# Non-local attention block: values to the output banks, outputs over six PSUM banks, pooled phi kept in theta's bank

## What is computed

```python
theta = jnp.einsum('bhwc,cd->bhwd', x, W_theta)            # 256 -> 32
phi = _maxpool2x2(jnp.einsum('bhwc,cd->bhwd', x, W_phi))   # 256 -> 32, pooled
g = _maxpool2x2(jnp.einsum('bhwc,cd->bhwd', x, W_g))       # 256 -> 128, pooled
theta = theta.reshape(B, S, Cc // 8)                       # S = 1024 pixels
phi = phi.reshape(B, Sk, Cc // 8)                          # Sk = 256 cells
g = g.reshape(B, Sk, Cc // 2)
beta = jax.nn.softmax(jnp.einsum('bqd,bkd->bqk', theta, phi), axis=-1)
tmp = jnp.einsum('bqk,bkv->bqv', beta, g).reshape(B, H, W, Cc // 2)
o = jnp.einsum('bhwv,vc->bhwc', tmp, W_o)
return gamma * o + x
```

## Time and profile before

| | us |
|---|---|
| median of 3 runs | 249.46 |
| lowest, highest | 247.31, 251.14 |
| the profiled execution | 248.0 |
| its span (first to last instruction) | 246.2 |
| TensorE busy | 235.7 (96%) |
| VectorE busy | 205.8 (84%) |
| GpSimd busy | 168.7 (69%) |
| ScalarE busy | 148.1 (60%) |

### The profile page before, as it was taken

One profiled execution on the slowest core, in us unless ns is written; L12 is line 12 of the kernel. 1 busy time (PEld: TensorE's weight loads), 2 busy tenths in 40 slices (PEclk: granted clock), 3 DMA queues, 4 the chain that ended last, 5 costly groups with the idle time before them and its releaser, 6 DMA issues.

```text
span 246.2 us, 4332 instructions
## 1 busy us (share of the span) xinstructions
PE 235.7 (96%) x1464; PEld 210.4 (85%) x1464; DVE 205.8 (84%) x473; ACT 148.1 (60%) x275; POOL 168.7 (69%) x119
## 2 busy tenths in 40 slices
PE   7896999999999999999999999999999999999884
PEld 4675888898989889898989989898998989899774
DVE  4587896988989898898989899898989989898855
ACT  3763865847475684847567484747749474735260
POOL 1596588676868677686958767695876779544480
PEclk9999999999999999999999999999999999999999
DMA  6790009549194775919377592928668391906924
GB/s 221 285 393 18 3 1 313 204 104 386 49 311 177 234 284 124 384 63 337 123 209 303 142 365 77 347 101 270 243 218 296 95 357 70 329 14 226 372 88 173
DMA packets 15078, 51.14 MB, mean 208 GB/s; under 512 B 1872, under 2 KB 2512, under 8 KB 15056
## 3 DMA queue, kind: packets, MB, share of 16 engines
q1 hardware_dynamic: 14368, 50.14, 58.2%
q10 hardware_dynamic: 688, 0.72, 0.8%
HBM read 33.95 MB, written 16.78 MB: 206 GB/s over the span
## 4 chain that ended last, share of the span: by engine, by line
PE 80%; DVE 7%; DMA 4%; ACT 3%; POOL 3%; issue 1%; ACTq 0%; DVEq 0%
PE proj L195 30%; PE out L299 24%; PE shift L299 8%; PE shift L272 6%; PE score L229 5%; PE score L256 4%; DVE neg_parts L577 3%; DMA x_t<-in_xt 2%; POOL e_lo L506 2%; DMA theta<-neg_lo 2%; PE shift L195 1%; DVE out L552 1%; DVE theta L558 1%; POOL x_lo L501 1%; PE proj L188 1%
## 5 line engine op out<-in xcount | busy, mean ns | idle before, releaser
L506 POOL TENSOR_TENSOR e_lo<-e_sb,e_hi 128x512 fp32r<-128x512 f32 x64 | 82.0, 1295 | 50.8 <-ACT e_sb L434 50.8
L501 POOL TENSOR_TENSOR x_lo<-x_t,x_hi 128x1024 fp32r<-128x1024 f32 x31 | 74.3, 2398 | 13.7 <-ACT x_hi L391 13.7
L299 PE MATMUL out<-G_hi,e_lo 128*128 128x258 f32 x188 | 53.2, 283 | 0.5 <-POOL e_lo L506 0.5
L299 PE MATMUL out<-G_hi,e_hi 128*128 128x258 f32 x188 | 53.4, 284 | 0.0
L299 PE MATMUL out<-G_lo,e_hi 128*128 128x258 f32 x188 | 53.3, 283 | 0.0
L603 DVE SCALAR_TENSOR_TENSOR y_sb<-out,r_sum,x_n 128x256 f32<-128x256 f32 x94 | 45.5, 484 | 6.4
L195 PE MATMUL proj<-x_hi,w_hi 128*128 128x512 f32 x122 | 48.4, 396 | 2.3 <-DVE theta L558 2.3
L195 PE MATMUL proj<-x_hi,w_lo 128*128 128x512 f32 x122 | 48.3, 396 | 0.0
L195 PE MATMUL proj<-x_lo,w_hi 128*128 128x512 f32 x122 | 48.2, 395 | 0.0
L431 ACT ACTIVATE e_hi<-shift 128x512 fp32r<-128x512 f32 x64 | 38.5, 601 | 13.5 <-PE shift L272 13.5
L577 DVE TENSOR_REDUCE neg_parts<-score 128x2 f32<-128x512 f32 x64 | 43.6, 685 | 1.3 <-PE score L229 0.4
(11 more groups left out here) (81 smaller groups left out, 386.3 us busy)
## 6 DMA issues: line engine op xcount, KB each, us to landing
x_n<-in_xn SPq DMA_DIRECT2D x32, 512.0 KB, 7.3
x_t<-in_xt SPq DMA_DIRECT2D x31, 512.0 KB, 5.3
out<-y_sb SPq DMA_DIRECT2D x31, 512.0 KB, 6.6
x_t<-in_xt ACTq DMA_DIRECT2D x2, 256.0 KB, 4.7
w_sb<-in_w_proj SPq DMA_DIRECT2D x1, 256.0 KB, 3.7
theta<-neg_hi ACTq DMA_DIRECT2D x16, 4.0 KB
theta<-neg_lo SPq DMA_DIRECT2D x16, 4.0 KB
out<-y_sb SPq DMA_DIRECT2D x1, 256.0 KB, 2.4
```

Of the source, the lines that this page charges most:

```text
L299: last = nc.tensor.matmul(out_bank(i, t)[:, 0:GW], e[:, i % 2, KC * h + k, cells], G[:, i % 3, k, :], start=(n == 0), stop=(n == 3 * KC - 1))
L501: nc.gpsimd.tensor_tensor(x_lo[:, i % 2, h], x_t[:, i % 2, h], x_hi[:, i % 2, h].bitcast(f32), ALU.subtract).then_inc(x_lo_ready, 1)
L506: nc.gpsimd.tensor_tensor(e_lo[:, i % 2, n, :], e_sb[:, n, :], e_hi[:, i % 2, n, :].bitcast(f32), ALU.subtract).then_inc(e_lo_ready, 1)
```

## The change

`values` go to `outb[h]` for all images but the first (before: `proj[h]`). The output tiles rotate over six banks (before: tiles 2 and 3 in `shift`, the others in `outb`). `mix` of images 0 and 1 goes to other banks. `phi_max` moves from rows 96 to 127 of `outb[1]` to rows 64 to 95 of `proj[0]`, where the third copy of theta was. Since ScalarE reads those rows in `theta_high`, `theta_low`, which waits for `theta_high`, is put ahead of `phi_pool` in VectorE's order. The waits of TensorE are written anew to fit the banks; `theta_phi` of image 1 and 2 waits for `phi_low` of the image before. No operation is added or taken away.

```diff
-        phi_max = outb[1][THETA:P, 0:NK]
+        phi_max = proj[0][2 * DK:THETA, 0:NK]
         LAST = B - 1
+        out_banks = (proj[1], shift[0], shift[1], proj[0], outb[0], outb[1], proj[1], outb[0])
 
         def value_bank(i, h):
-            return shift[h] if i == 0 else proj[h]
+            return shift[h] if i == 0 else outb[h]
 
         def mix_bank(i):
-            return outb[0] if i < 2 else proj[0] if i == LAST else score[0]
+            return shift[1] if i == 0 else outb[1] if i == 1 else proj[0] if i == LAST else score[0]
 
         def out_bank(i, t):
-            if i == LAST:
-                return (outb[0], outb[1], shift[0], shift[1])[t % 4]
-            return shift[t - 2] if t in (2, 3) else outb[t % 2]
+            return out_banks[t]
...
             def theta_phi(i, h):
-                if i == 1:
-                    pe.wait_ge(theta_lo_ready, h + 1)
-                    pe.wait_ge(phi_pooled, h + 1)
-                elif i > 1:
-                    pe.wait_ge(g_pooled, 2 * (i - 1) + h + 1)
+                if i in (1, 2):
+                    pe.wait_ge(theta_lo_ready, 2 * (i - 1) + h + 1)
+                    pe.wait_ge(phi_pooled, 2 * (i - 1) + h + 1)
+                    if h == 0:
+                        pe.wait_ge(phi_lo_ready, i)
+                elif i > 2:
+                    pe.wait_ge(y_ready, TILES * (i - 3) + (4 if h == 0 else 7))
...
             def values(i, h):
-                if i > 0:
-                    pe.wait_ge(theta_lo_ready, 2 * i + h + 1)
-                    pe.wait_ge(phi_pooled, 2 * i + h + 1)
+                if i == 2 and h == 0:
+                    pe.wait_ge(g_pooled, 3)
+                elif i == 2:
+                    pe.wait_ge(G_lo_ready, 2)
+                elif i > 2:
+                    pe.wait_ge(y_ready, TILES * (i - 3) + (8 if h == 0 else 6))
...
             def output(i, t):
                 h, w = divmod(t, HT)
+                later = i + 2
                 if t == 0:
-                    pe.wait_ge(G_lo_ready, max(i + 1, 2))
-                if t == 1 and real(i + 2):
-                    pe.wait_ge(phi_lo_ready, i + 3)
-                if t < 2:
-                    if i > 0:
-                        pe.wait_ge(y_ready, TILES * (i - 1) + 6 + t + 1)
-                elif t < 4:
-                    pe.wait_ge(e_ready, 4 * i + t + 1)
-                elif i == LAST:
-                    pe.wait_ge(y_ready, TILES * i + t - 4 + 1)
+                    pe.wait_ge(G_lo_ready, i + 1)
+                    if later < B:
+                        pe.wait_ge(theta_lo_ready, 2 * later + 2)
+                        pe.wait_ge(phi_pooled, 2 * later + 2)
+                    else:
+                        pe.wait_ge(y_ready, TILES * (i - 1) + 7)
+                elif t < 3:
+                    pe.wait_ge(e_ready, 4 * i + t + 2)
+                elif t == 3:
+                    if later < B:
+                        pe.wait_ge(phi_lo_ready, later + 1)
...
+                elif t < 6:
+                    if later < B:
+                        pe.wait_ge(g_pooled, 2 * later + t - 3)
+                    else:
+                        pe.wait_ge(y_ready, TILES * (i - 1) + (8 if t == 4 else 6))
                 else:
-                    pe.wait_ge(y_ready, TILES * i + (t - 4 if t < 6 else t - 2) + 1)
+                    pe.wait_ge(y_ready, TILES * i + (1 if t == 6 else 5))
...
             def phi_pool(i, h):
                 dve.wait_ge(tp_ready, 2 * i + h + 1)
-                if h == 0 and i >= 3:
-                    dve.wait_ge(y_ready, TILES * (i - 3) + TILES)
...
-            phi_pool(0, 0)
             theta_low(0, 0)
+            phi_pool(0, 0)
...
                 if s > 2:
                     for h in range(2):
+                        theta_low(a, h)
                         phi_pool(a, h)
-                        theta_low(a, h)
                         maxima(b, h)
```

More of the change, by code:

```diff
@@ L243, in mix @@
                     pe.wait_ge(wo_lo_ready, 1)
+                    pe.wait_ge(g_pooled, 2)
                 elif i == 1:
-                    pe.wait_ge(G_lo_ready, 1)
+                    pe.wait_ge(g_pooled, 4)
                 elif i == LAST:
-                    pe.wait_ge(g_pooled, 2 * i + 1)
+                    pe.wait_ge(y_ready, TILES * (i - 2) + 4)
                 else:
@@ L266, in shifted @@
                     if i > 0:
-                        pe.wait_ge(y_ready, TILES * (i - 1) + 2 + n + 1)
+                        pe.wait_ge(y_ready, TILES * (i - 1) + 1 + n + 1)
+                    elif n == 0:
+                        pe.wait_ge(g_pooled, 1)
                     else:
-                        pe.wait_ge(g_pooled, n + 1)
+                        pe.wait_ge(G_lo_ready, 1)
                 else:
@@ L277, in output @@
                 h, w = divmod(t, HT)
+                later = i + 2
                 if t == 0:
-                    pe.wait_ge(G_lo_ready, max(i + 1, 2))
-                if t == 1 and real(i + 2):
-                    pe.wait_ge(phi_lo_ready, i + 3)
-                if t < 2:
-                    if i > 0:
-                        pe.wait_ge(y_ready, TILES * (i - 1) + 6 + t + 1)
-                elif t < 4:
-                    pe.wait_ge(e_ready, 4 * i + t + 1)
-                elif i == LAST:
-                    pe.wait_ge(y_ready, TILES * i + t - 4 + 1)
+                    pe.wait_ge(G_lo_ready, i + 1)
[9 more added lines that the diff above has]
+                        pe.wait_ge(phi_lo_ready, later + 1)
+                    elif i == LAST - 1:
+                        pe.wait_ge(G_lo_ready, LAST + 1)
+                    else:
+                        pe.wait_ge(y_ready, TILES * (i - 1) + 4)
+                elif t < 6:
+                    if later < B:
+                        pe.wait_ge(g_pooled, 2 * later + t - 3)
+                    else:
+                        pe.wait_ge(y_ready, TILES * (i - 1) + (8 if t == 4 else 6))
                 else:
-                    pe.wait_ge(y_ready, TILES * i + (t - 4 if t < 6 else t - 2) + 1)
+                    pe.wait_ge(y_ready, TILES * i + (1 if t == 6 else 5))
                 cells = slice(P * w, P * (w + 1))
@@ L625, in finishes @@
                     finish(i, t)
+            theta_low(0, 0)
             phi_pool(0, 0)
-            theta_low(0, 0)
             g_pool(0, 0)
+            theta_low(0, 1)
             phi_pool(0, 1)
-            theta_low(0, 1)
             phi_low(0)
@@ L635, in _ @@
             maxima(0, 1)
+            theta_low(1, 0)
             phi_pool(1, 0)
-            theta_low(1, 0)
             maxima(0, 2)
@@ L646, in _ @@
             g_pool(1, 1)
+            theta_low(2, 0)
             phi_pool(2, 0)
-            theta_low(2, 0)
             maxima(1, 0)
+            theta_low(2, 1)
             phi_pool(2, 1)
-            theta_low(2, 1)
             G_low(1)
```

## The result

The changed kernel is slower: median of four executions 262.34 us (260.1 to 262.69), against 248.41 (247.31 to 251.14) for the kernel before, ratio 1.053 with a 95% interval of 1.0482 to 1.0578. Its profiled execution took 262.28 us with a span of 260.5, where before's took 248.0 with 246.2: 14.3 us more. The ratios here are formed without the few executions in a slower state of the chip, so they can differ a little from the quotient of the medians, which are those of all executions.

A forecast was written before the change was run, and what follows sets the result against it. Bound: a loop through VectorE's queue down to neg_low, its transfer and TensorE. 248.0 profiled + 8.8 (13 stages x 0.68) + 2.9 (start) = 259.7; put between this and the median's base, 260.4 us, range 254.5 to 264.5.

The forecast's parts named there:

- The loop through VectorE, the transfer and TensorE: Steady stage: projection end, VectorE's queue to neg_low, transfer, TensorE to next projection; 14.23 us, VectorE delays paid almost one for one.
- 0.60 late at theta_low, 0.68 at phi_low: Steady stage on VectorE: theta_low waits for ScalarE's theta copy, phi_low for later phi copies; 0.68 us lost per stage.
- The new pairs on VectorE don't close up, and pooling isn't longer: VectorE's swapped order: neighbours start no closer, pooling in one bank no slower; otherwise a stage loses 0.35 or 0.86, not 0.68.
- rival (a): VectorE's hand-overs partly free as new pairs close up, 0.35 a stage: 254.7 us, 256.2 with the median's offset; chance 0.10.
- TensorE's slack is about 0.18: Steady stage: TensorE's own path has only 0.18 us of slack against the loop through the transfer.
- Rival (b): TensorE is the bound, VectorE's 0.7 us of idle absorbs the copy, only the start is lost: 250.9 us; chance 0.09.
- turn_max's stall of 0.56 lies within the 0.68: Steady stage on TensorE: turn_max waits about 0.56 us for the last maxima, adding nothing to the 0.68 loss.
- The start costs 2.9: First images: theta_phi(1, 0) waits for phi_low(0), copies and poolings queue, mix(2) at about 40.1: 2.9 us, bounds 2.1 and 4.0.
- Rival (c): Not slower: freed waits of the start are the whole effect, new gate at theta_phi(1, 0) hidden: 245.7 us; chance 0.04.
- Rival (d): POOL becomes the gate: later x copies delay g_low, mix stops TensorE 0.3 more a stage: 263.6 us; chance 0.05.
- The transfer takes 1.82 in every stage: Steady stage: SyncE's small transfer of negated maxima, from issue at 122.19 to TensorE's weight load at 124.01, 1.82 us.
- Half of the median's offset, 0.7: Before's median stood 1.46 us above its profiled execution; the forecast was put between both bases, 260.4 instead of 259.7.

The follow-up runs named there:

- experiments two: Kernel before with the first maxima of a stage done twice from image 2 on, extra VectorE work ahead of neg_low: 257.07 us, ratio 1.0323.
- three: Kernel before with G_low done twice from image 2 on, extra VectorE work behind neg_low: 248.55 us, ratio 0.9981.
- nine: Kernel before with output tile 6 ahead of the shifted products and tiles 4 and 5 in the two projection banks: 246.4 us, ratio 0.9931.
- experiment one: Kernel before, every bank as it was, with theta_low put ahead of phi_pool on VectorE for images 3 to 15: 256.31 us, ratio 1.0292.
- experiment four: Changed kernel with pooled phi in SBUF, old VectorE order and no wait of theta_phi on phi_low for images 0 to 2: 259.51 us, ratio 1.0399.
- eight: Changed kernel with all pooled phi in SBUF, phi_pool first again and no waits on phi_low in theta_phi and output: 254.13 us, ratio 1.0181.
- experiment six: Changed kernel with output tile 6 ahead of the two shifted products on TensorE: 255.73 us, ratio 1.0287.
- experiments five: Changed kernel with neg_low ahead of the second finish on VectorE: 258.95 us, ratio 1.0427.
- twelve: Changed kernel run once more, unaltered: 264.23 us, ratio 1.0642.

## Why the prediction was right, and where it fell short

The forecast was 260.4 us, range 254.5 to 264.5, slower with 0.87. The time of 262.34 is in the range and on that side, 1.9 above the forecast. Step by step:

- *The loop through VectorE, the transfer and TensorE sets the stage.* Right. It was read from 0.30 us between two weight loads where no wait was listed, and experiments two, three and nine show it: 0.60 a stage ahead of neg_low, nothing behind, and a shorter stage once the transfer has slack.
- *0.60 late at theta_low, 0.68 at phi_low.* Measured 0.61 and 0.66; neg_low 0.65, stages 0.655 longer. 13 x 0.68 = 8.8 was 8.5. Swap and loss are one, by experiment one.
- *The new pairs on VectorE don't close up, and pooling isn't longer.* Right: theta_low to pooling 0.71, pooling to maxima 0.74, pooling 0.71 long beside 0.71 before. Both bounds (0.35 and 0.86) fall, and rival (a) with the lower. The Trainium skill's rule on held instructions, cited there, agrees.
- *New bank waits and the rotation are worth 0 in a stage.* Right: 14.91 without them, 14.90 with them.
- *TensorE's slack is about 0.18.* Right, a little large: its own stage is 14.09 where the loop had 14.23, so 0.14. Rival (b) falls by that.
- *turn_max's stall of 0.56 lies within the 0.68.* Right as a term (0.51 before its load, 13 times), incomplete as a reading: it is a loop of its own of about 14.6, so whoever repairs only the transfer's edge gets back 0.3 of 0.655 a stage. The sum didn't need that; a repair does.
- *The start costs 2.9.* theta_phi(1, 0) was to come at 16.25 and came at 16.18, theta_phi(2, 0) at 25.68 (25.6), the exponentials at 32.94 (33.2), mix(2) at 39.82 (40.1). Against before that is 2.63; but in this execution the second theta copy started 0.26 earlier (12.65, 12.91 in the earlier trace rows), so from the same point it is 2.89. Rival (c) falls here, by this and by experiment four.
- *GpSimd's margin of 0.3 holds.* Right: its g_low is listed as ending a wait of mix only at the start. Rival (d) falls.
- *The transfer takes 1.82 in every stage.* This is the term that was mis-sized. It was taken from one stage as a constant. In two of thirteen stages it took 3.27 and 3.65, together 3.4 us. The sum on the profile's basis was 259.7: less 0.3 (stages), 0.26 (the start's earlier copy) and 0.3 (the end), plus 3.4, gives 262.2, and 262.28 was measured. In the profile of before no steady stage had a late one. A term for it was missing, and with it some width upward: with a repetition whose median is 264.23 and one of whose executions took 265.75, the upper end of 264.5 was too low. It was so by the prediction's own terms: rival (d), 263.6, with the median's offset of 1.46 is 265.1.
- *Half of the median's offset, 0.7.* A fourth execution of before brought its median from 249.46 to 248.41, 0.4 over the profiled one. So it is partly luck that the forecast lies only 1.9 off: most of these 0.7 stand for an offset that wasn't there, and they covered a part of the 3.4 for the late transfers.

## What to carry to other kernels

Look for the loop that crosses the engines before trusting a busy share: go from a transfer's landing back to what issued it, and price an added wait by whether it lies ahead of that issue or behind it; the same 0.7 us cost 8 us in the one place and nothing in the other. When an edge is relieved, compute the next one, here turn_max at about 14.6, a bank at 14.33 and TensorE at 14.09, since a gain ends there. A move to another bank that forces a new order of two operations isn't a move alone: the order cost all of the 8.5 us in the stages, and two more banks for the output tiles gained once VectorE's order was left alone and TensorE's was changed to use them.

## What the hardware showed beyond expectation

**A 4 KB transfer beside an instruction fetch.** This is the DMA view of the changed kernel for the 1.8 us after the issue of a transfer that landed in time (130.2 to 132.0; queue and kind: packets, MB, share of 16 engines):

```profile
q8 instruction: 1, 0.02, 3.3%
q1 hardware_dynamic: 16, 0.00, 1.0%
q10 hardware_dynamic: 16, 0.00, 1.0%
```

and this for as long after the issue of the late one, 189.8 to 191.6:

```profile
q8 instruction: 1, 0.02, 3.0%
q10 hardware_dynamic: 16, 0.00, 1.0%
q1 hardware_dynamic: 14, 0.00, 0.9%
```

q10 carries ScalarE's small transfer, q1 SyncE's: eight packets of 512 bytes and eight of 4. Both stretches have a 16 KB packet of the instruction queue, but in the late one two of SyncE's sixteen are missing. Its eighth packet of 512 bytes starts 2.44 us after the issue, 0.02 before the instruction packet ends (its other seven start by 1.37), and the semaphore follows 1.2 us later; why so late isn't shown. In every late landing of images 2 to 13, in all the traces (nine, 2.08 to 3.65 us, in seven of the 14 traces), an instruction packet of 8 or 16 KB moved within the first 1.6 us after the issue, and in eight of the nine one 512-byte packet of the two small transfers (ScalarE's or SyncE's) starts 0.003 to 0.016 us before that packet's end. Thirty transfers in time have an instruction packet as well, which began between 0.3 us before and 1.6 after the issue, but no 512-byte packet of theirs is held. That the two stand on the same one of the 16 DMA engines explains this, and is an inference: the trace doesn't name the engine. The kernel's loads and stores don't explain a held packet here: at most three 4 KB packets of theirs start in the first 1.8 us, and up to five where the transfer was in time. For the last image, where loads run beside the transfer, they may. Two late ones of image 14 (2.27 and 2.05) had an instruction packet that began 0.3 before the issue. No experiment moved an instruction packet. The Trainium skill (Runtime: NRT & Kernel Launch, Instruction fetch mechanics) has instructions refilled in blocks of 16 KiB by a DMA queue and calls their cost mostly hidden. The 16 KB packets agree with the size (the 8 KB ones on q14 don't), and where a transfer with no slack meets one the cost here was 1.5 and 1.9 us.

**The port shared with GpSimd**: phi_low 0.42, 0.76 or 1.16 us long, by how long GpSimd's instruction beside it had still to run (experiments four and eight).

**The clock after one stall**: an idle of 2.16 or 2.17 us at the start, the new gate, stands in four traces. It was followed by the full clock in two (the changed kernel and experiment six) and by half of it in two (experiments five and twelve, granted clock 0.50 and 0.51), 1.25 us of difference. No trace with before's start has such a drop there, so the stall that the change adds may also add spread. Experiment four has none there either, but one earlier, from 8.5 to 11.9, so a drop in the start doesn't need the gate; the executions without a trace can't tell more.
